# Respreading the attention pieces of a gated attention + FFN kernel over the FFN's steps

## The reference

```python
# attention; x is the normed input here, k = v = the context
Q, K, V = x @ Wh, k @ Wh, v @ Wh                      # per head
masked = Q @ K.T / sqrt(128) * decay
A = maximum(abs(masked.sum(over the 64 blocks)), 1.0)
O = A @ V
Y = (O - mean(O)) / sqrt(var(O) + 1e-3) * gamma + beta
out = (relu(x @ wg) * Y) @ wo                         # W * Y @ wo
x1 = x + tanh(g_xattn) * out
# FFN, 11 x 128 = 1408 inner channels, ternary weights
h = silu(x2 @ gate.T * gate_s) * (x2 @ up.T * up_s)   # x2 = layernorm(x1)
result = x1 + tanh(g_ffn) * (h @ down.T) * down_s
```

## Time and profile before

| | us |
|---|---|
| three timed runs, median (lowest, highest) | 1690.33 (1687.54, 1690.52) |
| profiled execution, its own time | 1685.91 |
| its span | 1684.0 |
| TensorE matmuls busy | 1571.9 (93% of the span) |
| TensorE weight loads busy (beside the matmuls) | 1310.5 (78%) |
| VectorE busy | 958.0 (57%) |
| GpSimd busy | 668.7 (40%) |
| ScalarE busy | 474.3 (28%) |
| mean granted TensorE clock, share of full speed | 0.978 |

### The profile page before, as it was taken

One profiled execution on the slowest core, in us unless ns is written; L12 is line 12 of the kernel. 1 busy time (PEld: TensorE's weight loads), 2 busy tenths in 40 slices (PEclk: granted clock), 3 DMA queues, 4 the chain that ended last, 5 costly groups with the idle time before them and its releaser, 6 DMA issues.

```text
span 1684.0 us, 19980 instructions
## 1 busy us (share of the span) xinstructions
PE 1571.9 (93%) x7402; PEld 1310.5 (78%) x7402; DVE 958.0 (57%) x1492; ACT 474.3 (28%) x723; POOL 668.7 (40%) x749
## 2 busy tenths in 40 slices
PE   7999999998897988979889798898999999999999
PEld 5888888876776867768677686776888888888887
DVE  7677777776676767767667675774332232232232
ACT  4444444433212122121221212212223223222321
POOL 4455555514445455353554535533123113212311
PEclk9999999998999999999999999999999999999999
DMA  7777777657564765746647466563312321231220
GB/s 254 259 267 266 266 242 250 206 187 231 156 194 139 180 188 151 211 136 165 201 137 210 143 167 197 141 192 100 101 25 51 75 67 22 63 76 25 51 63 26
DMA packets 349155, 255.97 MB, mean 152 GB/s; under 512 B 257984, under 2 KB 259136, under 8 KB 348864
## 3 DMA queue, kind: packets, MB, share of 16 engines
q1 hardware_dynamic: 349056, 254.67, 50.7%
HBM read 156.05 MB, written 107.22 MB: 156 GB/s over the span
## 4 chain that ended last, share of the span: by engine, by line
PE 78%; DVE 8%; POOL 8%; issue 3%; DMA 2%; ACT 1%; SPq 0%; DVEq 0%; ACTq 0%
PE ps L1161 45%; PE pyb L1061 17%; PE ps L1096 5%; PE po L1061 5%; PE ptb L1061 5%; POOL wyt L996 4%; POOL reg L1000 3%; PE ptb L1066 2%; POOL reg L992 1%; DVE tmp L770 1%; DVE misc L716 1%; DVE xbuf L760 1%; DVE xn L749 1%; ACT reg L521 1%; DMA raw<-v_scratch 1%
## 5 line engine op out<-in xcount | busy, mean ns | idle before, releaser
L1000 POOL TENSOR_TENSOR reg<-tmp,reg 128x512 fp32r<-128x512 f32 x176 | 236.1, 1342 | 514.9 <-ACT reg L521 514.9
L1161 PE MATMUL ps<-reg,gate 128*128 128x512 f32 x1408 | 350.4, 391 | 0.0
L1161 PE MATMUL ps<-reg,up 128*128 128x512 f32 x1408 | 347.7, 389 | 0.0
L1161 PE MATMUL ps<-xreg,reg 128*128 128x512 f32 x1408 | 324.2, 389 | 0.0
L770 DVE SCALAR_TENSOR_TENSOR tmp<-ps,colsb,tmp 128x512 f32<-128x512 f32 x176 | 131.0, 744 | 322.9 <-PE ps L1161 304.1
L1161 PEld LDWEIGHTS ps<-reg,up 128*128 128x128 f32 x1408 | 264.4, 188 | 54.8
L1161 PEld LDWEIGHTS ps<-reg,gate 128*128 128x128 f32 x1408 | 263.2, 189 | 55.8 <-DVE reg L764 2.3
L1161 PEld LDWEIGHTS ps<-xreg,reg 128*128 128x128 f32 x1408 | 263.9, 188 | 54.4
L531 ACT ACTIVATE tmp<-ps,colsb 128x512 f32<-128x512 f32 x176 | 121.1, 688 | 398.9 <-PE ps L1161 398.9
L964 POOL TENSOR_SCALAR rs<-mv 128x1 f32<-128x1 f32 x192 | 48.6, 253 | 456.3 <-DVE mv L739 176.0
L521 ACT CAST reg<-tmp 128x512 fp32r<-128x512 f32 x176 | 109.3, 621 | 375.3 <-DVE tmp L770 375.3
(11 more groups left out here) (103 smaller groups left out, 1641.6 us busy)
## 6 DMA issues: line engine op xcount, KB each, us to landing
xr<-in_x SPq DMA_DIRECT2D x63, 512.0 KB, 5.4
raw<-in_ctx_t SPq DMA_DIRECT2D x32, 512.0 KB, 4.6
w_scratch<-tmp SPq DMA_DIRECT2D x64, 256.0 KB, 3.9
v_scratch<-tmp SPq DMA_DIRECT2D x64, 256.0 KB, 3.7
raw<-v_scratch SPq DMA_DIRECT2D x32, 512.0 KB, 4.7
raw<-w_scratch SPq DMA_DIRECT2D x64, 256.0 KB, 3.6
x_scratch<-xr SPq DMA_DIRECT2D x32, 512.0 KB, 3.7
xr<-x_scratch SPq DMA_DIRECT2D x32, 512.0 KB, 5.4
```

Source lines behind the costliest of these rows:

```text
L1000: e.tensor_tensor(hid[1][:, m % 11, :], tmp[:, m % 3, :], f(hid[0][:, m % 11, :]), ALU.subtract).then_inc(s["hlo"])
L1161: last = e.matmul(dst, l, r, start=(k == 0 and i == 0), stop=(k == n - 1 and i == 1))
```

## The change

- A pair's pieces are spread over 13 steps where there were 10. The first piece starts earlier (`first_step`), W*Y's low part becomes piece 7, the product with wo piece 9, the second norm 10, its two transposes 10 and 11, and its store 12.
- The first Y work of a pair is put in pieces 0 to 3, one block at a time: `y_second` and `wy_blocks` of block t are piece 2, of block t+1 piece 3.
- W*Y is stored a tile at a time (`wy_out(t)`, 256 KB each, with a semaphore for each tile), so that the even tile can go out a step earlier; `wy_in` waits for both.
- Loads for later pairs (`w_load`, `v_load`, `x_again`) move in SP's queue with them.
- `silu` is issued ahead of the pieces on ScalarE. In group 0 the x2 pairs are fetched later, as the first pairs are finished later.

The core of the diff; its hunks after `pieces` are of SP (to `x2_in`), ScalarE (`v_hi(3)`, ahead of the loop), VectorE (`y_stats(5)`, ahead of the loop, and the pieces up to `stats2`), GpSimd and TensorE:

```diff
 def first_step(q):
-    return 15 * (q - 2) // 4 - 1
+    return 15 * (q - 3) // 4 + 1 if q > 2 else -2
 def pieces(n):
-    return [(q, n - first_step(q)) for q in range(2, B // 2) if 0 <= n - first_step(q) <= 9]
+    return [(q, n - first_step(q)) for q in range(2, B // 2) if 0 <= n - first_step(q) <= 12]
...
-            def wy_out(q):
-                p.wait_ge("wyb", 2 * q - 2)
-                if q > 2:
-                    p.wait_ge("wyl", 64 * (q - 2))
-                e.dma_start(wy_s.rearrange("t p n -> p t n"), tbuf).then_inc(s["wys"], 16)
+            def wy_out(t):
+                p.wait_ge("wyb", t - 3)
+                if t >= 6:
+                    p.wait_ge("wyl", 64 * (t // 2 - 2))
+                e.dma_start(wy_s[t % 2], tbuf[:, t % 2, :]).then_inc(s[f"wys{t % 2}"], 16)
...
             def wy_in(q):
-                p.wait_ge("wys", 16 * (q - 1))
+                p.wait_ge("wys0", 16 * (q - 1))
+                p.wait_ge("wys1", 16 * (q - 1))
...
+                        if piece == 12:
+                            x2_out(q)
+                            x1_store(q)
                         if piece == 3:
-                            wy_out(q)
+                            wy_out(2 * q)
                             if q + 1 < B // 2:
                                 w_load(2 * q + 2)
-                                w_load(2 * q + 3)
-                            wy_in(q)
                             if q + 2 < B // 2:
                                 v_load(q + 2)
                         if piece == 4:
+                            wy_out(2 * q + 1)
+                            if q + 1 < B // 2:
+                                w_load(2 * q + 3)
+                            wy_in(q)
+                        if piece == 6:
                             x_again(q)
-                        if piece == 9:
-                            x2_out(q)
-                            x1_store(q)
-                    if g + 1 < NG and step in (9, 12):
-                        x2_in(2 * g + (2 if step == 9 else 3))
+                    if g + 1 < NG and step == (9 if g else 11):
+                        x2_in(2 * g + 2)
+                    if g + 1 < NG and step == (12 if g else 14):
+                        x2_in(2 * g + 3)
...
+            v_hi(3)
...
+            y_stats(5)
+            y_scaled(5)
...
-                        if piece == 8:
+                        if piece == 11:
+                            x2_blocks(t + 1)
+                        if piece == 10:
                             norm2(t)
                             norm2(t + 1)
                             x2_blocks(t)
-                            x2_blocks(t + 1)
-                        if piece == 2:
-                            wy_blocks(t)
-                            y_second(t + 1)
-                            wy_blocks(t + 1)
-                        if piece == 1:
-                            y_stats(t + 1)
-                            y_scaled(t + 1)
-                            y_second(t)
+                        if piece in (2, 3):
+                            y_second(t + piece - 2)
+                            wy_blocks(t + piece - 2)
...
-                        if piece == 7:
+                        if piece == 9:
                             x1(t)
                             stats2(t)
                             x1(t + 1)
                             stats2(t + 1)
...
-                        if piece == 6:
+                        if piece == 7:
                             wy_pair_lo(q)
-                        if piece == 7:
+                        if piece == 9:
                             rstd2(2 * q)
                             rstd2(2 * q + 1)
...
-                            if piece == 7:
+                            if piece == 9:
                                 wo_mm(2 * q, range(4))
                                 wo_mm(2 * q + 1, range(4))
```

More of the change, by code:

```diff
@@ L14 @@
     + [f"{name}{i}" for name in ("ct", "vst", "wst", "wl", "xa", "x1s", "res", "out") for i in range(2)]
-    + ["wys", "wyl", "x2s", "x2l"]
+    + ["wys0", "wys1", "wyl", "x2s", "x2l"]
     + [f"scr{c}" for c in range(12)] + [f"wld{c}" for c in range(8)]
@@ L607, in _ @@
                         hidden_hi(11 * g + step - 1)
+                    if step < 11:
+                        silu(g, step)
                     for q, piece in pieces(15 * g + step):
@@ L612, in _ @@
                             wy_pair_hi(q)
[L613 to L616, removed]
+                    if g + 1 < NG and step == (11 if g else 12):
+                        x2_pair_hi(2 * g + 2)
+                    if g + 1 < NG and step == (13 if g else 14):
+                        x2_pair_hi(2 * g + 3)
         @block.vector
@@ L708, in y_scaled @@
                 else:
[L709 removed]
+                    p.wait_ge(f"wys{t % 2}", 16 * (t // 2 - 2))
                 e.scalar_tensor_tensor(halves(y_to(t)), po[:, :, t % 2, :], mv[:, t % 8, 0:1], halves(gamma), ALU.subtract,
@@ L933, in _ @@
                             x2_blocks(t)
-                            x2_blocks(t + 1)
-                        if piece == 2:
-                            wy_blocks(t)
-                            y_second(t + 1)
-                            wy_blocks(t + 1)
-                        if piece == 1:
-                            y_stats(t + 1)
-                            y_scaled(t + 1)
-                            y_second(t)
+                        if piece in (2, 3):
+                            y_second(t + piece - 2)
+                            wy_blocks(t + piece - 2)
                     for q, piece in pieces(15 * g + step):
                         t = 2 * q
-                        if piece == 0:
-                            y_stats(t)
-                            y_scaled(t)
-                        if piece == 7:
+                        if piece in (0, 1):
+                            y_stats(t + piece)
+                            y_scaled(t + piece)
+                    for q, piece in pieces(15 * g + step):
+                        t = 2 * q
+                        if piece == 9:
                             x1(t)
@@ L952, in _ @@
                             stats2(t + 1)
-                    if g + 1 < NG and step in (11, 14):
-                        x2_pair_lo(2 * g + (2 if step == 11 else 3))
+                    if g + 1 < NG and step == (11 if g else 12):
+                        x2_pair_lo(2 * g + 2)
+                    if g + 1 < NG and step == 14:
+                        x2_pair_lo(2 * g + 3)
             finish(B - 1)
@@ L1037, in _ @@
             y_rstd(4)
+            y_rstd(5)
             for g in range(NG):
```

## The result

The changed kernel takes 1616.07 us (median of four runs, 1614.61 to 1616.94) against 1690.34 before: a ratio of 0.9563, 95% interval 0.9547 to 0.9580. The forecast was 1616. Its profiled execution takes 1615.26 us, with a span of 1613.5 and a mean granted clock of 0.991.

The account below looks back on a forecast made before the run. TensorE's waits, mainly for W*Y's low part, and slow matmuls behind them were taken to bound the kernel. 1685.9 less 133.0 lost, plus 61 lost after (18.9, 35.0, 4 and 3), plus 2 gave 1616 us, range 1590 to 1640.

Parts of the forecast that it names:

- What was lost before: TensorE's FFN part before the change: 789.6 us taken for 656.6 of work, 94.5 in waits and 38.5 in slow matmuls.
- The wait for the low part of W*Y goes: Two steps, 8.7 us at the tightest, cover the 5.9 to 8.1 needed before wo, giving back 88.4 us.
- A: TensorE's o ahead of step 4 waits 2.3 us for V's low part in seven groups; 18.9 us with slow matmuls.
- B: Step 0 waits 3.6 us for `x2_pair_lo` in seven groups, VectorE slowed by GpSimd's shared port; 35.0 us with slow matmuls.
- C: At the start, o ahead of step 1 waits 2.4 us for V's low part; 4 us with slow matmuls.
- Slow matmuls: TensorE matmuls running slower behind a wait: 38.5 us lost before, 1.6 us behind each of 24 long waits.
- The time: Profiled execution 1685.9 us less 133.0 plus 61 gives 1613.9; 2 us added for the median, 1616.
- Rival 1: Step 0's wait without the port is 1.3 us, no slow matmuls, 9 instead of 35 us: 1590 us; chance 0.12.
- Rival 2: The low parts still come late for TensorE, 43 us: 1659 us, or 1638 at half of that; chance 0.13.
- Rival 3: x2's second pair, behind W*Y's transfers in SP's queue, lands 25 us late and holds step 0: 1701 us; chance 0.03.
- Rival 4: Two W*Y stores each have a fixed part, about 2 us; 28 pairs lose up to 1 us: 1644; chance 0.02.
- The rest costs nothing, by its cover: W*Y's split stores, `wy_in`, x2's transfer and the later norm and store are covered by steps between, costing TensorE nothing.

Follow-up runs that it names:

- e6: Kernel before the change, with the product with wo and what follows it one piece later (piece 8), old spread and single store kept: 1635.65 us.
- e2: Changed kernel with GpSimd's low part of V issued ahead of `hidden_lo` in its step: 1609.36 us.
- e4: Changed kernel with GpSimd's low part of W*Y held in step 0, from group 1 on, until x2's second low part is done: 1592.84 us.
- e12: e6 with GpSimd's low part of V issued ahead of `hidden_lo` in its step: 1613.12 us.
- e1: Changed kernel with the low part of x2's second pair issued right behind `finish` in VectorE's step 14, from group 1 on: 1604.27 us.
- e3: Changed kernel with the edits of e1 and e2 together: 1590.67 us.
- e8: e3 with the stores of x2 and x1 issued behind W*Y's stores of the same step in SP's queue: 1573.49 us.
- e9: Changed kernel with only the stores of x2 and x1 issued behind W*Y's stores of the same step in SP's queue: 1616.26 us.

## Why the prediction was right

**What was lost before, 133.0 us.** The sum rests on the prices of the earlier trace rows. They hold after the change too: by them 61.6 us are lost there, where the forecast had 61. One small reading was off: the 2.3 us for `x2_pair_lo` are waits of the weight loads, TensorE's matmuls list none, so they belong to the slow matmuls. The sum of both is the same.

**The wait for the low part of W*Y goes.** Right: 0.3 us where it was 88.4. The 0.6 us to spare in the worst case were used up once, by 0.3 us. e6 shows that the second step alone takes the wait away.

**A.** Forecast 2.3 us seven times; measured 2.10 six times and, in group 0, 3.41 once, 16.0 us against 16.1. e2 shows that it is the place of V's low part in GpSimd's step. That the sum is so near is in part luck: the longer wait in group 0 was not foreseen.

**B.** Forecast 3.6 us seven times; measured 3.47. The mechanism, GpSimd's instruction holding the two-input and norm instructions of VectorE, is shown by e4, which leaves 1.40 us where 1.3 was forecast. Its detail held too: L791 lost 0.13 us and the norms 2.08, and the forecast had nearly all of it in the norms.

**C.** Forecast 2.4 us, measured 2.60.

**Slow matmuls.** 14.2 us forecast in A, B and C and 3 for what I had not found; measured 18.4 us in all. By the distances of the rows' starts, B's share is 10.7 us (about 1.75 behind six of the waits, 0.2 behind one; forecast 9.8), the start's 1.75 (1.6), and A's 2.4 (2.8). But A's are not spread as forecast: 1.7 stand behind the one long wait, and each of the six of 2.10 us has 0.1.

**The time.** The profiled execution was to take 1613.9 us and took 1615.26. The median was to be 2 us above it and is 0.8, so that 1616 against 1616.07 is nearer than the method deserves.

**Rivals.** Rival 1 (B without the port) is excluded by e4's 3.47 to 1.41 us. Rival 2 (low parts late again) is there as a tendency, 0.3 us once, and becomes real in e2 (4.9 us) and e12 (9.6). Rival 3's transfer never decided anything: in e1 `x2_pair_lo` stands earlier in the step, right behind `finish`, and no wait for a DMA stands ahead of it in its timeline. Rival 4 was the wrong way round: the split gains 6.7 us. What the Trainium skill gives in the section that the prediction names (DMA: Bandwidth & Descriptors, Anatomy of one DMA) is measured on DMAs issued by GpSimd; these are SP's, and no run here shows the fixed part by itself.

**The step that failed**, without harm to the sum, is "The rest costs nothing, by its cover", for the stores. The cover I named was that of the data's readers; what is not covered is `y_scaled`, which writes the tile anew and must wait for the store to land: 18.7 us in the changed kernel, 42.9 in e3, where it cost 17 us (1590.67 to 1573.49 in e8).

## What to carry to other kernels

When work is moved in in-order queues, price each wait as "end of the step's chain on the slow engine minus the time at which TensorE is back", and do it again at the places where the moved work was the cover of something else: here this gave both new waits within 0.2 us. It fails where the chain begins late: e6's 4.7 us were 7.44, as `hidden` was taken at its best. Look at what runs beside it on the engine that shares a port, since one instruction there made a step two microseconds longer here. And expect a fix to gain only the distance to the next wait: e1 and e2 gave 12 and 7 us singly, with the stores' order 43 us together, and that order alone gave nothing.

## What I had not expected of the hardware

- A `norm2` of 0.54 us alone took up to 2.65 us beside GpSimd's two-input instruction, and in e1 `x2_pair_lo`, 1.18 us alone, took 3.41. VectorE's transposes (L769) kept their 0.70 us in all 60 rows, one of them beside `hidden_lo` (881.82).
- A 256 KB store with 1 MB ahead of it in the same queue landed 9 us after its issue (in e1); the median for such a store in this kernel is 3.3 us.
- Behind a wait of TensorE of 2.10 us, o took 1.69 us in all six rows of this kind in the changed kernel (1.59 without a wait), but 2.93 us in two of six in e9 and in one in e4. What tells them apart no run here shows.
